# A four-part graph network kernel: gathers of two layers start with the landed table, biases move from one-row products to additions, a split is shared with ScalarE

## The chip, the cores and the metric

One Trainium2 chip, of which the kernel uses one core: TensorE (PE, with its weight loads PEld), VectorE (DVE), ScalarE (ACT), GpSimd (POOL) and SyncE (SP, which issues most transfers), with SBUF and PSUM. The metric is the device time of one execution in microseconds.

## The reference

Four graph layers, each added to a residual x (6250 nodes of 128 features) behind a layer norm and a ReLU, over 106,250 edges (src, dst) sorted by dst:

```
x = x + L0(h)   # hypergraph attention, two conv layers l = 0, 1: xt = x@W; softmax over hyperedges;
                #   eout = segment_sum(m1, col); nout = segment_sum(m2, row); out = LN(nout + bias)*gamma + beta
                #   x = tanh(out + x)
x = x + L1(h)   # messages relu([x[row], x[col]] @ mW1 + mb1) @ mW2 + mb2, segment_sum to col,
                #   relu(relu([x, agg] @ uW1 + ub1) @ uW2 + ub2)
x = x + L2(h)   # gated edge messages with an inner layer norm, segment_sum, upd @ W_out + b_out
x = x + L3(h)   # two graph attentions, edges forwards and backwards
```

Here h = relu(layer_norm(x)) before each part.

## The kernel before

Nodes lie in 49 blocks (NB) of 128, handled in 13 GROUPS of up to four blocks. X, H and ACC hold 49 blocks of 128 features in SBUF: the residual, the layer's input and the sums. Edges lie in 928 tiles of 128; four tiles make one of 232 groups (NG).

The program is a row of stages, and the edge sweeps among them are ORDER = "abafcdee": a, b, a, f are the two conv layers of L0 (l = 0: a to the hyperedges, b back to the nodes; l = 1: a again, then f, which also reads kept one-hots and bits from memory), c is L1, d is L2, e twice is L3. This text calls the two a sweeps a0 and a2. Ahead of each sweep a short stage makes a table of transformed rows in memory:

- l0_sp, l0_pe, l0_ac, l0_ve (lines 1871 to 1953): the table tab[TW] of conv layer l. SP loads five weights and biases into WT (lines 1872 to 1877; both layers use the same place, so layer 1's loads wait for the stage to begin) and stores 13 groups (L1886). PE's first product (L1892) waits for all five.
- l0_mid (1961 to 1987): between a and b (or a and f); makes the hyperedges' means, stored to memory by L1981 in one transfer; DVE clears ACC (L1977).
- l0_end (1989 to 2040): DVE multiplies each of four parts of blocks (PARTS) by gamma (L2008), adds beta (L2009), adds H (L2010), ACT takes the tanh; three norm statistics and ACT's normalisation (L585) go in turns with it.
- l1_sp, l1_pe, l1_ac, l1_ve (2059 to 2112): L1's table tab[256] (13 stores, L2068) and, in SBUF, the rows for the destination side, which DVE splits into three bfloat16 parts per group (mb1 added by L2109, then the four instructions of split_ve, L658 to L661). SP loads w1, w2, u1, u2 and three biases at its beginning (L2060 to L2065); PE's first product and DVE wait for all seven.
- u_pe, u_ve, u_ac (2140 to 2214): L1's update network; l2_* (2218 to 2271): L2's tables and a spill of X to memory (L2220, 1792 KB); v_pe, v_ve (2279 to 2324): L2's output product. In u and v the product with u2 or Wo is followed by a product of one row that adds the bias (times1, 2121 to 2126).

In a sweep, rows_po (L618 to L623) has POOL issue four indirect gathers per group (one tile each: 128 table rows) into a ring of groups: 10 deep in a, 8 in b, f and c. POOL waits only for the semaphore that says a ring place has been read (S.r; in a it is ACT's L899 that reads it). DVE makes one-hot matrices, PE sums by them, DVE adds the sums to ACC.

Between stages all five engines meet: each drains, counts up s_met and waits until all five have done so (pass_by counts up without waiting, and own makes an engine wait for its own last instruction):

```python
def meet(eng):
    met[eng.engine] = met.get(eng.engine, 0) + 1
    eng.drain().then_inc(s_met, 1)          # L152
    eng.wait_ge(s_met, 5 * met[eng.engine])
def pass_by(eng):
    met[eng.engine] = met.get(eng.engine, 0) + 1
    eng.drain().then_inc(s_met, 1)
```

An idle stretch that the profile ends with L152 so ended with another engine's arrival at such a meeting. There is a meeting between l0 and a, two between a and b or f, and one between l1 and c. At the first a, credit_po (L467), a set of GpSimd stores of its own, comes between l0 and the sweep.

Of the kernel before, what the change touches and what calls it, by code (L numbers as in the profile page):

```python
# [10 lines left out]
ALU = mybir.AluOpType  # L11
# [91 lines left out]
def build(nc, a, out):  # L103
# [5 lines left out]
    with ctx:  # L109
# [915 lines left out]
        def b_po(po, p):  # L1025
            at, ring = raised_before(p)
# [82 lines left out]
        def f_po(po, p):  # L1109
            at, ring = raised_before(p)  # L1110
# [116 lines left out]
        def c_po(po, p):  # L1227
            meet(po)
# [623 lines left out]
        Wc0, att = WT[:, 0:130], WT[:, 130:132]  # L1852
        bia, gam, bet = (WT[:, 140 + 128 * i:268 + 128 * i] for i in range(3))
# [16 lines left out]

        def l0_sp(sp, l):
            sp.dma_start(Wc0[:, 0:128], a["L0_gnn_W"][l]).then_inc(s_w0, 16)
            sp.dma_start(att, a["L0_gnn_att"][l].rearrange("(c p) -> p c", p=128),
                         allow_slow_non_contiguous=True).then_inc(s_w0, 16)
            sp.dma_start(bia, bcast(a["L0_gnn_bias"][l], 128)).then_inc(s_w0, 16)
            sp.dma_start(gam, bcast(a["L0_gnn_gamma"][l], 128)).then_inc(s_w0, 16)
            sp.dma_start(bet, bcast(a["L0_gnn_beta"][l], 128)).then_inc(s_w0, 16)
# [9 lines left out]
            for i in range(NGR - 4, NGR):  # L1887
                stored(sp, l, i)

        def l0_pe(pe, l):  # L1890
            pe.wait_ge(s_w0, 80 * (l + 1))
            pe.transpose(PS[:, 7, 0:128], Wc0[:, 0:128], ident[:, :]).then_inc(s_wt, 1)  # L1892
            pe.wait_ge(s_wtc, l + 1)
            pe.matmul(PS[:, 7, 0:2], W0t, att, start=True, stop=True).then_inc(s_wp, 1)
            z = N0 * l
            for t in range(N0 + 1):
# [7 lines left out]
                if t >= 1:  # L1904
# [5 lines left out]
                    if i >= 2:  # L1910
                        pe.wait_ge(s_ts, z + i - 1)
                    times(pe, wide(2 + 2 * (i % 2), n, w), n,
                          [(wk512(i % 2), Wc0[:, 0:129] if w == 129 else Wc0[:, 129:130])]).then_inc(s_pr, 1)

        def l0_ac(ac, l):
# [3 lines left out]
            for t in range(N0):  # L1919
# [4 lines left out]
                ac.activation(wk512(t % 2)[:, 0:128 * n], PS[:, t % 2, 0:128 * n], ACT.Copy).then_inc(s_ht, 1)  # L1924

        def l0_ve(ve, l):
# [6 lines left out]
            ve.tensor_copy(Wc0[:, 128:130], PS[:, 7, 0:2]).then_inc(s_wc, 1)  # L1933
# [55 lines left out]
        def l0_end_ve(ve, l):  # L1989
# [5 lines left out]
            def summed(i):  # L1995

                lo, hi = PARTS[i]
                for b in range(lo, hi):
                    last = ve.scalar_tensor_tensor(A[:, b, :], A[:, b, :], S2[:, b:b + 1], bia, ALU.mult, ALU.add)
# [3 lines left out]
            def added(i):  # L2003
# [4 lines left out]
                own(ve, "ve", ve.tensor_tensor(P, P, rep(gam, hi - lo), ALU.mult))  # L2008
                own(ve, "ve", ve.tensor_tensor(P, P, rep(bet, hi - lo), ALU.add))  # L2009
# [44 lines left out]
        SQT, SQU = (B2[:, 9420 + 512 * i:9932 + 512 * i].rearrange("p (b c) -> p b c", c=128) for i in range(2))  # L2054
# [4 lines left out]
        def l1_sp(sp):  # L2059
            sp.dma_start(c2(w1), two(a["L1_gnn_mW1"])).then_inc(s_w1, 16)  # L2060
            sp.dma_start(w2, a["L1_gnn_mW2"]).then_inc(s_w1, 16)
            sp.dma_start(c2(u1), two(a["L1_gnn_uW1"])).then_inc(s_w1, 16)
# [9 lines left out]
        def l1_pe(pe):  # L2072
            for t in range(NGR + 1):
# [29 lines left out]

        def l1_ve(ve):
# [11 lines left out]
        s_np = sem("normed_part")  # L2116
# [3 lines left out]

        def times1(pe, outs, n, HT, w, bias):

            for k in range(n):
                pe.matmul(outs[:, k, :], HT[:, 128 * k:128 * k + 128], w, start=True, stop=False)
                mm = pe.matmul(outs[:, k, :], one_row, bias[0:1, :], start=False, stop=True)
            return mm
# [13 lines left out]
        def u_pe(pe):  # L2140

            for t in range(NGR + 3):
# [17 lines left out]
                if f := staged(t, 3):  # L2160
# [4 lines left out]
                    times1(pe, slim(6 + i % 2, n), n, uDH[i % 2], u2, ub2).then_inc(s_ur, 1)  # L2165
# [19 lines left out]
        def u_ve(ve):  # L2185

            for t in range(NGR + 3):
# [73 lines left out]
        def l2_ve(ve):  # L2261

            for i, (b0, n) in enumerate(GROUPS):
# [5 lines left out]
                ve.tensor_tensor(SB[:, b0:b0 + n, :], wide(4, n, 256), rep(bsr[1], n), ALU.add).then_inc(s_tb2, 1)  # L2269

# [8 lines left out]
        def v_pe(pe):  # L2279
            for t in range(NGR + 1):  # L2280
# [5 lines left out]
                if f := staged(t, 1):  # L2286
# [4 lines left out]
                    times1(pe, slim(2 + i % 2, n), n, vH[i % 2], Wo, bob).then_inc(s_up, 1)  # L2291
# [403 lines left out]
```

## Time and profile before

| | us |
|---|---|
| median of the runs (3; 11420.74 to 11429.36) | 11423.58 |
| the profiled execution | 11428.81 |
| its span, first to last instruction | 11427.0 |
| POOL busy in it | 7501.8 (66%) |
| PE busy / PE weight loads | 8042.8 (70%) / 5923.8 (52%) |
| DVE busy | 7905.9 (69%) |
| ACT busy | 5676.6 (50%) |
| granted TensorE clock, mean | 0.688 |

A share over the whole span says little here, since the stages have different limits. The sweeps are a 1024 to 2192 us, b 2237 to 3405, a2 3517 to 4677, f 4720 to 5882, c 6040 to 7205, d 7335 to 8712, and the two e behind 8853; between them lie the short stages named above. A clock of 1.00 is TensorE at 2.4 GHz and 0.50 at 1.2 GHz; a value between them is a mean over a stretch that has both.

### The profile page before, as it was taken

The numbers are of one execution on the slowest core, as the hardware profiler recorded it, in microseconds if no ns is written. First come the engines' busy times: TensorE is split into PE (matmuls) and PEld (weight loads), VectorE is DVE, ScalarE is ACT, GpSimd is POOL, SyncE is SP. The second block draws the span as 40 slices with busy tenths as digits, with TensorE's granted clock in tenths as the row PEclk, the third lists the DMA queues.
The fourth block names the chain that finished last, engine by engine and source line by source line (L and its number), as shares of the span: only waits on it lengthen the run. The fifth ranks groups of instructions, "written<-read, shape, count | busy, mean of one in ns | idle before, by whom it ended". The sixth has DMA issues, their size and how long they took to land. (4 is left out here: it accounts for less than half of the span.)

```text
span 11427.0 us, 187407 instructions
## 1 busy us (share of the span) xinstructions
PE 8042.8 (70%) x47078; PEld 5923.8 (52%) x47078; DVE 7905.9 (69%) x33260; ACT 5676.6 (50%) x17089; POOL 7501.8 (66%) x7674
## 2 busy tenths in 40 slices
PE   7895777666665777666645555888888777767776
PEld 5674444444444444444434555666666444444444
DVE  8766888744447888644453222588886799979998
ACT  4553555454444555455551111366665566646665
POOL 2444777677775777677756777466663677747775
PEclk8776666655556666555557777899998666666666
DMA  1112222255652222488954444355553544444443
GB/s 17 9 20 50 55 55 55 65 136 135 136 127 56 56 55 55 126 215 212 211 140 130 131 131 131 109 155 154 154 153 100 136 139 138 138 116 139 139 137 114
DMA packets 713309, 1294.48 MB, mean 113 GB/s; under 512 B 197090, under 2 KB 369216, under 8 KB 711872
## 3 DMA queue, kind: packets, MB, share of 16 engines
q0 software_dynamic: 282368, 575.57, 24.7%
q1 hardware_dynamic: 389520, 612.10, 16.8%
q10 hardware_dynamic: 40368, 94.82, 2.1%
q8 instruction: 411, 6.73, 0.2%
q14 instruction: 642, 5.26, 0.2%
HBM read 1048.44 MB, written 233.37 MB: 112 GB/s over the span
## 5 line engine op out<-in xcount | busy, mean ns | idle before, releaser
L623 POOL DMA_INDIRECT WK<-tab,IDX x4640 | 4411.9, 951 | 1702.9 <-issue 1372.3
L1637 POOL DMA_INDIRECT B<-tab,IDX x1856 | 1780.2, 959 | 710.8 <-issue 529.2
L623 POOL DMA_INDIRECT H<-tab,IDX x928 | 880.2, 949 | 539.2 <-DVE H L1441 261.6
L1767 ACT ACTIVATE B<-B 128x33 f32<-128x33 f32 x5568 | 1210.7, 308 | 7.9
L1656 DVE TENSOR_REDUCE WK<-PS 128x4 f32<-128x1024 f32 x928 | 1130.3, 1219 | 91.7 <-PE PS L1782 85.2
L926 PE MATMUL PS<-B 128*128 128x130 f32 (+1 forms) x3712 | 777.7, 374 | 393.2 <-ACT B L899 393.1
L1815 PEld LDWEIGHTS PS<-B,H 128*128 128x128 f32 x3712 | 829.2, 333 | 377.5 <-issue 372.2
L1815 PE MATMUL PS<-B,H 128*128 128x132 f32 x3712 | 893.6, 435 | 177.3 <-DVE ACC L1669 177.3
L1782 PE MATMUL PS<-WK,B 27*128 27x512 bf16 x1856 | 690.0, 481 | 396.0 <-DVE WK L1656 386.7
L926 PEld LDWEIGHTS PS<-B 128*128 128x128 f32 x3712 | 661.8, 268 | 581.6 <-ACT B L899 581.6
L887 ACT ACTIVATE B<-PS,PICK 18x512 bf16<-18x512 f32 x464 | 357.3, 770 | 1138.2 <-PE PS L944 1116.3
L1243 DVE TENSOR_TENSOR WK<-PS,WK 128x512 f32<-128x512 f32 x232 | 160.4, 692 | 840.0 <-DMA WK<-tab,IDX 826.1
L985 PE MATMUL PS<-WK,B 128*128 128x129 f32 x1856 | 381.0, 370 | 509.2 <-ACT WK L1287 366.5
L463 POOL DMA_INDIRECT pieces<-WK,B x208 | 353.4, 1699 | 574.4 <-ACT WK L451 294.6
L1022 ACT ACTIVATE B<-WK 128x128 f32<-128x128 f32 x1856 | 588.7, 388 | 237.9 <-ACT B L698 93.6
L1287 ACT ACTIVATE WK<-WK 128x512 f32<-128x512 f32 x232 | 146.5, 631 | 968.6 <-DVE WK L1243 968.6
L985 PE MATMUL PS<-B 128*128 128x129 f32 x1856 | 467.8, 430 | 222.6 <-ACT B L1022 222.2
L985 PEld LDWEIGHTS PS<-WK,B 128*128 128x128 f32 x1856 | 329.7, 267 | 555.7 <-issue 555.1
L899 ACT ACTIVATE B<-WK 128x128 f32<-128x128 f32 x1856 | 584.6, 385 | 0.0
L985 PE MATMUL PS<-B,WK 128*128 128x129 f32 x1856 | 474.1, 435 | 138.0 <-ACT B L1022 135.4
L397 PEld LDWEIGHTS PS<-B,WK 128*128 128x128 f32 x3328 | 487.7, 234 | 115.1 <-issue 100.9
L985 PEld LDWEIGHTS PS<-B 128*128 128x128 f32 x1856 | 403.6, 320 | 274.0 <-ACT B L1022 273.4
(476 smaller groups left out, 19980.9 us busy)
## 6 DMA issues: line engine op xcount, KB each, us to landing
H<-onehots SPq DMA_DIRECT2D x232, 768.0 KB
B<-onehots SPq DMA_DIRECT2D x232, 384.0 KB
onehots<-B ACTq DMA_DIRECT2D x232, 384.0 KB
WK<-tab,IDX POOLq DMA_INDIRECT x4640
onehots<-WK SPq DMA_DIRECT2D x232, 256.0 KB
B<-onehots SPq DMA_DIRECT2D x232, 256.0 KB
WK<-onehots SPq DMA_DIRECT2D x232, 256.0 KB
onehots<-B SPq DMA_DIRECT2D x232, 128.0 KB
```

Source lines behind the costliest of these rows:

```text
L397: mm = pe.matmul(PS[:, 4 + x % 2, 64 * (t // TC):64 * (t // TC) + 64], OHL[x % 2][:, t, :], PROD[x % 2][:, t, :, :].rearrange("p i w -> p ...
L623: po.indirect_dma_start(out=G[:, g % n, k, :], out_offset=None, in_=table, in_offset=bass.IndirectOffsetOnAxis(ap=IDX[:, idx, t:t + 1], ax ...
L887: ac.activation(aETb[:, r % 2, :], PS[0:18, 2 + r % 2, :], ACT.Identity, bias=abi[0:18, :], scale=asc[0:18, :]).then_inc(S.n1, 1)
L899: i = ac.activation(aR[:, r % 2, k, 0:128], aG[:, g % 10, k, 0:128], ACT.Copy, scale=aEW[:, r % 2, k:k + 1])
L926: mm = pe.matmul(aAG(r, k // 2)[:, 0:n], aOH[:, g % 10, k, :], aR[:, r % 2, k, 0:n], start=k % 2 == 0, stop=k % 2 == 1)
L985: mm = pe.matmul(AG(r, k // 2), OH[:, r, k, :], R[:, r % n, k, 0:129], start=k % 2 == 0, stop=k % 2 == 1)
L1022: i = ac.activation(bR[:, r % 2, k, 0:128], bG[:, r, k, 0:128], ACT.Copy, scale=bEW[:, r % 2, k:k + 1])
L1637: po.indirect_dma_start(out=eG[:, g % 5, k, :], out_offset=None, in_=tab[TW3], in_offset=bass.IndirectOffsetOnAxis(ap=IDX[:, o, t:t + 1], ...
L1656: ve.tensor_reduce(eM2[:, g, b:b + 2, 2 * i:2 * i + 2, 1] if isinstance(g, int) else eM2[:, bass.ds(g, 1), b:b + 2, 2 * i:2 * i + 2, 1].re ...
L1767: i = ac.activation(eR[:, q, k, 33 * h:33 * h + 33], eG[:, g % 5, k, 33 * h:33 * h + 33], ACT.Copy, scale=eEX[:, r, 4 * k + h:4 * k + h + 1])
L1782: mm = pe.matmul(PS[:, b + h, :], eSEL[:, b + h, :], eET[:, r, 512 * i:512 * i + 512], start=True, stop=True)
L1815: mm = pe.matmul(eAG(k // 2), eSTo[:, r, k // 4, 128 * (k % 4):128 * (k % 4) + 128], eR[:, r % 2, k, 0:132], start=k % 2 == 0, stop=k % 2 ...
```

## The change

- In a, b, f and c, POOL passes the meeting by and waits for the stores of the table (the last four of the 13, or the one of the means). One meeting of all engines per l0, and the one behind l1, go. credit_po moves into l0. The tiles HT0 of l0 move out of the memory that the gathers fill.
- L0's weights have a place for each layer; layer 1's are loaded at the end of layer 0's l0_sp. L1's w1, w2 and u1 are loaded in f's SP program at its ninth group; PE waits for these three alone.
- beta is added to H in four parts during b and f (shifted_ve), no longer to ACC in l0_end.
- In l1, DVE only adds mb1 per group, into ACC. Afterwards ACT makes eight copies and DVE eight subtractions over quarters of the blocks, in turns, and DVE clears ACC at the end; before, the clearing stood at the start.
- times1 becomes times. In u DVE adds ub2 in PSUM ahead of the ReLU; in v's place DVE adds bob to X in four parts during l2, and X's spill goes behind the eleventh store of l2.

The diff, cut to its core:

```diff
@@ f_sp
+                if g == 8:
+                    sp.dma_start(c2(w1), two(a["L1_gnn_mW1"])).then_inc(s_w1, 16)
+                    sp.dma_start(w2, a["L1_gnn_mW2"]).then_inc(s_w1, 16)
+                    sp.dma_start(c2(u1), two(a["L1_gnn_uW1"])).then_inc(s_w1, 16)
         def a_po(po, p):
-            meet(po)
+            pass_by(po)
+            for i in range(NGR - 4, NGR):
+                stored(po, p // 2, i)
             at, ring = raised_before(p)
...
         def b_po(po, p):
+            pass_by(po)
+            po.wait_ge(s_eod, 16)
             at, ring = raised_before(p)
...
+        def shifted_ve(ve, j, l):
+
+            if j in (24, 32, 40, 48):
+                lo, hi = PARTS[j // 8 - 3]
+                ve.wait_ge(s_w0, 80 * (l + 1))
+                ve.tensor_tensor(H[:, lo:hi, :], H[:, lo:hi, :], rep(bet[l], hi - lo), ALU.add)
...
             def body(j, u):
+                shifted_ve(ve, j, 0)
...
         def f_po(po, p):
+            pass_by(po)
+            po.wait_ge(s_eod, 32)
...
             def body(j, u):
+                shifted_ve(ve, j, 1)
...
         def c_po(po, p):
-            meet(po)
+            pass_by(po)
+            for i in range(NGR - 4, NGR):
+                stored(po, 2, i)
...
+        w0 = [WT[:, 756 * l:756 * l + 524] for l in range(2)]
+        HT0 = [B2[:, 8000 + 512 * i:8512 + 512 * i] for i in range(2)]
...
         def l0_sp(sp, l):
-            sp.dma_start(Wc0[:, 0:128], a["L0_gnn_W"][l]).then_inc(s_w0, 16)
...
-            sp.dma_start(bet, bcast(a["L0_gnn_beta"][l], 128)).then_inc(s_w0, 16)
+            if l == 0:
+                l0_weights_sp(sp, 0)
...
             for i in range(NGR - 4, NGR):
                 stored(sp, l, i)
+            if l == 0:
+                l0_weights_sp(sp, 1)
@@ l0_end_ve
-                own(ve, "ve", ve.tensor_tensor(P, P, rep(gam, hi - lo), ALU.mult))
-                own(ve, "ve", ve.tensor_tensor(P, P, rep(bet, hi - lo), ALU.add))
+                own(ve, "ve", ve.tensor_tensor(P, P, rep(gam[l], hi - lo), ALU.mult))
@@ l1_pe
-                    pe.wait_ge(s_w1, 112)
+                    pe.wait_ge(s_w1, 48)
...
+        def split_ac(ac):
+
+            ac.wait_ge(s_sq1, NGR)
+            for q, i in ((0, 0), (1, 0), (0, 1), (2, 0), (1, 1), (3, 0), (2, 1), (3, 1)):
+                whole, p, rest = sq_part(q)
+                if i:
+                    ac.wait_ge(s_sb, (1, 2, 4, 6)[q])
+                ac.activation(p[i], rest if i else whole, ACT.Copy).then_inc(s_sa, 1)
+
         def l1_ve(ve):
-            ve.memset(flat(ACC[:, :, :]), 0.0)
             ve.wait_ge(s_w1, 112)
             for i, (b0, n) in enumerate(GROUPS):
                 ve.wait_ge(s_ta1, i + 1)
-                ve.tensor_tensor(SQT[:, 0:n, :], wide(2 + 2 * (i % 2), n, 256)[:, :, 128:256], rep(mb1, n),
+                ve.tensor_tensor(ACC[:, b0:b0 + n, 0:128], wide(2 + 2 * (i % 2), n, 256)[:, :, 128:256], rep(mb1, n),
                                  ALU.add).then_inc(s_sq1, 1)
-                ve.wait_ge(s_sq1, i + 1)
-                split_ve(ve, lambda k: SQ3[:, b0:b0 + n, k, :], SQT[:, 0:n, :], SQU[:, 0:n, :])
+            for q, last_ in ((0, 0), (1, 0), (0, 1), (2, 0), (1, 1), (3, 0), (2, 1), (3, 1)):
+                whole, (p0, p1, p2), rest = sq_part(q)
+                if last_:
+                    ve.wait_ge(s_sa, (3, 5, 7, 8)[q])
+                    ve.tensor_tensor(p2, rest, p1, ALU.subtract).then_inc(s_sb, 1)
+                else:
+                    ve.wait_ge(s_sa, (1, 2, 4, 6)[q])
+                    if q >= 2:
+                        ve.wait_ge(s_sb, (3, 5)[q - 2])
+                    ve.tensor_tensor(rest, whole, p0, ALU.subtract).then_inc(s_sb, 1)
+            own(ve, "ve", ve.memset(flat(ACC[:, :, :]), 0.0))
@@ u_pe, v_pe
-                    times1(pe, slim(6 + i % 2, n), n, uDH[i % 2], u2, ub2).then_inc(s_ur, 1)
+                    times(pe, slim(6 + i % 2, n), n, [(uDH[i % 2], u2)]).then_inc(s_ur, 1)
...
-                    times1(pe, slim(2 + i % 2, n), n, vH[i % 2], Wo, bob).then_inc(s_up, 1)
+                    times(pe, slim(2 + i % 2, n), n, [(vH[i % 2], Wo)]).then_inc(s_up, 1)
@@ u_ve
-                    ve.scalar_tensor_tensor(X[:, b0:b0 + n, :], slim(6 + i % 2, n), 0.0, X[:, b0:b0 + n, :], ALU.max,
+                    F = slim(6 + i % 2, n)
+                    own(ve, "ve", ve.tensor_tensor(F, F, rep(ub2, n), ALU.add))
+                    ve.scalar_tensor_tensor(X[:, b0:b0 + n, :], F, 0.0, X[:, b0:b0 + n, :], ALU.max,
@@ l2_sp, l2_ve
-            sp.wait_ge(s_ux, NGR)
-            sp.dma_start(xs[:, 128 * XK:], xf[:, 128 * XK:]).then_inc(s_xs, 16)
...
+                if i == 10:
+                    sp.wait_ge(s_bob, 4)
+                    sp.dma_start(xs[:, 128 * XK:], xf[:, 128 * XK:]).then_inc(s_xs, 16)
...
+                if i in (3, 5, 7, 9):
+                    lo, hi = PARTS[(i - 3) // 2]
+                    ve.wait_ge(s_np, (i - 3) // 2 + 1)
+                    ve.tensor_tensor(X[:, lo:hi, :], X[:, lo:hi, :], rep(bob, hi - lo), ALU.add).then_inc(s_bob, 1)
@@ @block.gpsimd (one meet less per l0 layer on each other engine too, and one behind l1)
-                meet(po)
                 if l == 0:
+                    po.wait_ge(s_ts, 1)
                     credit_po(po)
                 a_po(po, 2 * l)
-                meet(po)
                 meet(po)
```

## Rows read from the trace of the kernel before

**Rows 1.** Windows a0, b, c, u, d, v: PE, PEld, DVE, ACT, POOL; clock; DMA.

```profile
1024.00:2192.00 1168.00, 840.52 (x5026) 559.95 (x5026) 979.64 (x6400) 595.44 (x1818) 885.18 (x928) 0.65 0.25 55
2237.00:3405.00 1168.00, 767.80 (x3920) 542.00 (x3920) 529.09 (x3233) 581.11 (x1612) 885.17 (x927) 0.52 0.59 135
6040.00:7205.00 1165.00, 652.62 (x4784) 592.81 (x4785) 285.96 (x715) 153.51 (x247) 882.14 (x928) 0.73 0.47 132
7214.70:7287.60 72.90, 71.62 (x420) 57.47 (x420) 44.49 (x182) 29.57 (x64) 9.43 (x5) 0.93 0.06 26
7390.00:8748.90 1358.90, 1134.43 (x6745) 932.38 (x6744) 1214.00 (x4798) 885.38 (x2031) 838.43 (x885) 1.00 0.51 151
8766.00:8851.30 85.30, 85.16 (x265) 62.25 (x265) 35.95 (x169) 22.34 (x51) 7.84 (x4) 0.50 0.13 50
```

**Rows 2.** Timeline of POOL, first gathers: start, us, instruction [idle before <-releaser].

```profile
1024.23 1.16 POOL L623 DMA_INDIRECT WK<-tab,IDX  x1 [79.40 <-SPq L152]
...
2237.24 1.00 POOL L623 DMA_INDIRECT WK<-tab,IDX  x1 [44.35 <-DVEq L152]
...
3517.36 1.06 POOL L623 DMA_INDIRECT WK<-tab,IDX  x1 [63.70 <-SPq L152]
...
6040.23 1.02 POOL L623 DMA_INDIRECT WK<-tab,IDX  x1 [58.61 <-DVEq L152]
```

**Rows 3.** Timeline of SP's queue: the stores ahead of a0, b, a2, c.

```profile
984.70 13.14 SPq L1886 DMA_DIRECT2D tab<-WK  x10
...
2221.75 0.36 SPq L1981 DMA_DIRECT2D tab<-ACC  x1
...
3481.25 18.17 SPq L1886 DMA_DIRECT2D tab<-WK  x13
...
6000.55 33.26 SPq L2068 DMA_DIRECT2D tab<-WK  x13
```

**Rows 4.** DMA issues: xcount, KB each, median us to landing.

```profile
tab<-WK SPq DMA_DIRECT2D x24, 264.0 KB, 3.0
...
tab<-ACC SPq DMA_DIRECT2D x2, 1650.0 KB, 8.3
...
tab<-WK SPq DMA_DIRECT2D x12, 256.0 KB, 2.3
```

**Rows 5.** Waits of PE in a0, DVE in b, f, c: total us, times, longest.

```profile
PE PS L944 <- DMA WK<-tab,IDX: 33.7, 61, 2.4
...
DVE WK L1052 <- DMA WK<-tab,IDX: 562.7, 227, 5.5
...
DVE B L704 <- DMA bits<-B: 385.7, 210, 6.9
...
DVE WK L1243 <- DMA WK<-tab,IDX: 826.1, 228, 7.5
```

**Rows 6.** Timeline of DVE at a0's start, of PE at the second l0's.

```profile
1023.38 3.45 DVE L854 TENSOR_SCALAR B<-iof,LOW 128x128 f32<-128x128 f32 x16 [3.93 <-SPq L152]
...
3474.47 0.45 PE L1892 MATMUL PS<-ident,WT 128*128 128x128 f32 x1 [60.31 <-DMA WT<-in_L_gnn_beta]
```

**Rows 7.** Groups of DVE instructions in the first l0_end: busy us, mean ns.

```profile
L2009 DVE TENSOR_TENSOR ACC<-ACC,WT 128x1536 f32<-128x1536 f32 (+1 forms) x4 | 7.2, 1791 | 0.1
```

**Rows 8.** Groups of instructions in l1, its products on PE.

```profile
L1845 PE MATMUL PS<-WT,WK 128*128 128x256 f32 x98 | 26.1, 412 | 11.4 <-DMA WT<-in_L_gnn_ub 4.9 <-ACT WK L2095 4.2 <-DVE B L2109 2.3
```

**Rows 9.** Timeline of PE in u: a block with its bias, products without.

```profile
7241.06 0.48 PE L2125 MATMUL PS<-WT,IDX 1*128 1x128 f32 x2
...
7241.89 0.48 PE L2125 MATMUL PS<-WT,IDX 1*128 1x128 f32 x2
...
7244.46 1.06 PE L1845 MATMUL PS<-WT,WK 128*128 128x128 f32 x8
```

**Rows 10.** Timeline of DVE in v: two groups.

```profile
8800.01 0.69 DVE L2319 TENSOR_TENSOR X<-X,PS 128x512 f32<-128x512 f32 x1 [0.94 <-PE PS L2125]
...
8806.54 0.69 DVE L2319 TENSOR_TENSOR X<-X,PS 128x512 f32<-128x512 f32 x1 [4.65 <-PE PS L2125]
```

More of the change, by code:

```diff
@@ L1849, in wk512 @@
             return WK[:, 512 * i:512 * i + 512]
-        Wc0, att = WT[:, 0:130], WT[:, 130:132]
-        bia, gam, bet = (WT[:, 140 + 128 * i:268 + 128 * i] for i in range(3))
+        w0 = [WT[:, 756 * l:756 * l + 524] for l in range(2)]
+        Wc0, att = [w[:, 0:130] for w in w0], [w[:, 130:132] for w in w0]
+        bia, gam, bet = ([w[:, 140 + 128 * i:268 + 128 * i] for w in w0] for i in range(3))
+        HT0 = [B2[:, 8000 + 512 * i:8512 + 512 * i] for i in range(2)]
         W0t = wk512(2)[:, 0:128]
@@ L1869, in stored, with l0_weights_sp @@
             eng.wait_ge(s_st[m % 4], 16 * (m // 4 + 1))
-        def l0_sp(sp, l):
-            sp.dma_start(Wc0[:, 0:128], a["L0_gnn_W"][l]).then_inc(s_w0, 16)
[L1873 to L1876, printed above, removed]
-            sp.dma_start(bet, bcast(a["L0_gnn_beta"][l], 128)).then_inc(s_w0, 16)
+        def l0_weights_sp(sp, l):
+            sp.dma_start(Wc0[l][:, 0:128], a["L0_gnn_W"][l]).then_inc(s_w0, 16)
+            sp.dma_start(att[l], a["L0_gnn_att"][l].rearrange("(c p) -> p c", p=128),
+                         allow_slow_non_contiguous=True).then_inc(s_w0, 16)
+            sp.dma_start(bia[l], bcast(a["L0_gnn_bias"][l], 128)).then_inc(s_w0, 16)
+            sp.dma_start(gam[l], bcast(a["L0_gnn_gamma"][l], 128)).then_inc(s_w0, 16)
+            sp.dma_start(bet[l], bcast(a["L0_gnn_beta"][l], 128)).then_inc(s_w0, 16)
+        def l0_sp(sp, l):
+            if l == 0:
+                l0_weights_sp(sp, 0)
             sp.wait_ge(s_rfc, l + 1)
@@ L1888, in l0_sp @@
                 stored(sp, l, i)
+            if l == 0:
+                l0_weights_sp(sp, 1)
         def l0_pe(pe, l):
             pe.wait_ge(s_w0, 80 * (l + 1))
-            pe.transpose(PS[:, 7, 0:128], Wc0[:, 0:128], ident[:, :]).then_inc(s_wt, 1)
+            pe.transpose(PS[:, 7, 0:128], Wc0[l][:, 0:128], ident[:, :]).then_inc(s_wt, 1)
             pe.wait_ge(s_wtc, l + 1)
-            pe.matmul(PS[:, 7, 0:2], W0t, att, start=True, stop=True).then_inc(s_wp, 1)
+            pe.matmul(PS[:, 7, 0:2], W0t, att[l], start=True, stop=True).then_inc(s_wp, 1)
             z = N0 * l
@@ L1912, in l0_pe @@
                     times(pe, wide(2 + 2 * (i % 2), n, w), n,
-                          [(wk512(i % 2), Wc0[:, 0:129] if w == 129 else Wc0[:, 129:130])]).then_inc(s_pr, 1)
+                          [(HT0[i % 2], Wc0[l][:, 0:129] if w == 129 else Wc0[l][:, 129:130])]).then_inc(s_pr, 1)
         def l0_ac(ac, l):
@@ L1923, in l0_ac @@
                     ac.wait_ge(s_pr, z + t - 1)
-                ac.activation(wk512(t % 2)[:, 0:128 * n], PS[:, t % 2, 0:128 * n], ACT.Copy).then_inc(s_ht, 1)
+                ac.activation(HT0[t % 2][:, 0:128 * n], PS[:, t % 2, 0:128 * n], ACT.Copy).then_inc(s_ht, 1)
         def l0_ve(ve, l):
@@ L1932, in l0_ve @@
             ve.wait_ge(s_wp, l + 1)
-            ve.tensor_copy(Wc0[:, 128:130], PS[:, 7, 0:2]).then_inc(s_wc, 1)
+            ve.tensor_copy(Wc0[l][:, 128:130], PS[:, 7, 0:2]).then_inc(s_wc, 1)
             z = N0 * l
@@ L1998, in summed @@
                 for b in range(lo, hi):
-                    last = ve.scalar_tensor_tensor(A[:, b, :], A[:, b, :], S2[:, b:b + 1], bia, ALU.mult, ALU.add)
+                    last = ve.scalar_tensor_tensor(A[:, b, :], A[:, b, :], S2[:, b:b + 1], bia[l], ALU.mult, ALU.add)
                 own(ve, "ve", last)
@@ L2053, in build @@
         SQ3 = SQP.rearrange("p (b i c) -> p b i c", i=3, c=128)
-        SQT, SQU = (B2[:, 9420 + 512 * i:9932 + 512 * i].rearrange("p (b c) -> p b c", c=128) for i in range(2))
+        SQU = B2[:, 9420:9420 + 25 * 128].rearrange("p (b c) -> p b c", c=128)
         TS1 = [wk512(4 + i).rearrange("p (b c) -> p b c", c=128) for i in range(4)]
@@ L2059, in l1_sp @@
         def l1_sp(sp):
-            sp.dma_start(c2(w1), two(a["L1_gnn_mW1"])).then_inc(s_w1, 16)
-            sp.dma_start(w2, a["L1_gnn_mW2"]).then_inc(s_w1, 16)
-            sp.dma_start(c2(u1), two(a["L1_gnn_uW1"])).then_inc(s_w1, 16)
             sp.dma_start(u2, a["L1_gnn_uW2"]).then_inc(s_w1, 16)
@@ L2102, in l1_ac, with sq_part @@
                                   ACT.Copy).then_inc(s_ta1, 1)
+        s_sa, s_sb = sem("split_copied"), sem("split_rest")
+        def sq_part(q):
+            lo, hi = PARTS[q]
+            return ACC[:, lo:hi, 0:128], [SQ3[:, lo:hi, i, :] for i in range(3)], SQU[:, 12 * (1 - q % 2):12 * (1 - q % 2) + hi - lo, :]
+        def split_ac(ac):
[5 more added lines that the diff above has]
+                ac.activation(p[i], rest if i else whole, ACT.Copy).then_inc(s_sa, 1)
         def l1_ve(ve):
-            ve.memset(flat(ACC[:, :, :]), 0.0)
             ve.wait_ge(s_w1, 112)
@@ L2119, in build @@
                  14: (2, 0, 4), 15: (2, 4, 8), 16: (2, 8, 12)}
[L2121 to L2126, printed above, removed]
         def normed_ac(ac, n, q, lo, hi):
@@ L2509, in _ @@
                 meet(po)
-            meet(po)
             c_po(po, 4)
@@ L2543, in _ @@
                     bits_ve(ve)
-                meet(ve)
                 a_ve(ve, 2 * l, l)
@@ L2553, in _ @@
             l1_ve(ve)
-            meet(ve)
             c_ve(ve, 4)
@@ L2575, in _ @@
                 l0_ac(ac, l)
-                meet(ac)
                 a_ac(ac, 2 * l)
@@ L2584, in _ @@
             l1_ac(ac)
-            meet(ac)
+            split_ac(ac)
             c_ac(ac, 4)
@@ L2616, in _ @@
                     pick_pe(pe)
-                meet(pe)
                 a_pe(pe, 2 * l, l)
@@ L2624, in _ @@
             l1_pe(pe)
-            meet(pe)
             c_pe(pe, 4)
@@ L2649, in _ @@
                 meet(sp)
-                meet(sp)
                 l0_mid_sp(sp, l)
@@ L2659, in _ @@
             l1_sp(sp)
-            meet(sp)
             meet(sp)
```

2 lines of the change are left out of this document (1 added, 1 removed).

## The prediction

> **What bounds the kernel now.** I read the table of stages first [rows 1]. In the five sweeps that the change touches, GpSimd issues 928 gathers, and the stage takes about 928 times one gather's pitch: 1168 us over 928 is 1.26 us. No other engine is full there: DVE, the next in a0, is busy 980 of 1168 us, TensorE 841. The list of who waits then agrees [rows 5]: in c DVE waits 826 us for gathers, in b 563. So the end of such a sweep is the first gather plus about 1168 us, and what counts is when that first gather starts. Next come the GpSimd rows at each start [rows 2]: it stands idle for 44 to 79 us until a drain of the meeting (L152) of SyncE or VectorE, not until data. Between sweeps, short stages are bound by other things: u and v by TensorE [rows 1], layer 1's table by DVE's split and by its weights.
>
> **Gathers begin with the landed table.** Each stage: last store's issue, its landing, and the distance to the first gather.
> - a0: the last store of the table is issued by 984.70 + 13.14 = 997.8 [rows 3] and lands 3.0 us later [rows 4]: 1000.9. The first gather is at 1024.23 [rows 2]. Gain **23.3**. The consumers get less: DVE's first one-hots start at 1023.38 after 3.93 us for that meeting [rows 6], most of it GpSimd's credit stage, now done earlier: about 3.9 sooner. The gathers so run 19.4 us (four groups of 5.03, 1168 over 232) further ahead into a ring of ten. In the steady state TensorE waits only 33.7 us in 61 waits for gathers [rows 5], so the consumers keep pace with little to spare; their own slack, 980 of 1168 us on DVE, is some 0.4 us per group at most, enough to win 19 us back over 50 to 100 of the 232 groups. I take the full 23.3, with 3.9 as the lower bound (the ring full from the start and never caught up).
> - b: one store of the means is issued at 2221.75 + 0.36 and lands after 8.3 [rows 3, 4]: 2230.4, against the first gather at 2237.24: **6.5**, after a little for the wait. The meeting here waits for DVE's clearing of the accumulators; the consumers have half their time idle [rows 1, 5] and follow.
> - a2: stores end 3481.25 + 18.17 + 3.0 = 3502.4 against 3517.36: **14.5**, bounds 4 and 15 as in a0.
> - f: built as b and worth 6.5 at its start, but DVE waits 386 us in 210 waits for the kept bits from memory [rows 5], so gathers aren't alone in setting its end. I take **3** of -2 to 6.5.
> - c (layer 1): three things in one start. Before, the first gather is 6040.23 and the 13 stores run from 6000.55 for 33.26 us [rows 2, 3]: 12 steps of 2.77 us, paced by the DVE split that frees PSUM. With the split behind the stage TensorE paces it: 26.1 us of its products by 13 groups is 2.0 us [rows 8], some of it at the lower clock, 2.16 with the transposes: 12 x 0.61 = 7.3. The weights, loaded in f, no longer hold TensorE for 4.9 [rows 8]. The last landing (6033.8 + 2.3 [rows 4]) is 4.1 ahead of the first gather, 0.5 of which stays: 3.6. Sum **15.8**, bounds 11 and 17. What it adds lies in c's beginning: eight ACT copies and eight DVE subtractions of about 1.8 us each (as L2009's tiles, [rows 7]), alternating, and a clearing of 6517 elements, 7 us at L2009's pace (an estimate), that stood in the weights' shadow. c's consumers start 7 us later than now, so 23 us further behind the gathers, under the 40 us that the ring of eight holds; with 826 us of waiting in c they catch up within ten groups. If that cover were gone, it would cost those 7.
>
> **Weights of layer 1 of the hypergraph, loaded early.** TensorE's first product stands until 3474.47 for the last of five loads [rows 6]; the meeting is over at about 3467.7. About 1.1 of it remains: **5.7** (3 to 6.8). SyncE issues the same five loads behind a0's stores, where its queue has nothing due.
>
> **Norm's shift in the passes.** L2009 is four additions of 1.79 us [rows 7] in each of two ends, a chain of DVE and ACT in turns. Half of 7.2 lies on the path: **3.6 each, 7.2 in all** (3.6 to 14). The additions now stand in b and f, where DVE waits 563 and 386 us [rows 5]; without that cover they'd cost 7.2 each.
>
> **One-row products.** In u TensorE is busy 71.6 of 72.9 us [rows 1]. The products with a bias take 0.83 us per block (two passes and two one-row passes), while eight products without a bias take 1.06 [rows 9]: per group 3.3 becomes about 1.0. DVE becomes the bound: 44.5 us busy [rows 1] and 13 more additions of 0.69 (a pass over such a tile, [rows 10]) are 53.5, with fill and tail 59: gain 14. Layer 2's table then gets four additions of 1.8 us in DVE's gaps (cover: its stage is bound by TensorE), and the spill of X (1792 KB; a store of 1650 KB lands in 8.3 us [rows 4]) moves ahead of the last two stores: -1 to -3. I take **11** (0 to 15). In v the clock was 0.50 throughout and a group takes 6.53 us [rows 1, 10]; with 4 transposes and 8 products it is about 2.8 (an estimate: 1.06 doubled and 0.7), DVE with its statistics 3.1: 13 groups make 40, with fill and the last statistics 47 instead of 86: 39. The table stage behind may then see more of the low clock, 0 to 19: I take **36** (20 to 41).
>
> **The sum.** 23.3 + 6.5 + 14.5 + 3 + 15.8 + 5.7 + 7.2 + 11 + 36 = **123 us**. The profiled execution took 11428.8 us (span 11427.0 and 1.8 around it), 5 us over the median of 11423.6. 11428.8 - 123 is 11306, the median's own 11301; I say **11304**. The terms at their low ends give about 3.9 + 6 + 4 - 2 + 11 + 3 + 3.6 + 0 + 20 = 50, at their high ends about 145.
>
> **The rivals.**
> 1. **The head start is given back in a0 and a2.** For it: TensorE's waits for gathers there are short, and the granted clock of 0.65 isn't fixed; a ring that fills puts the end on the consumers, and only their 3.9 and 4 count. Against: gathers run at their pitch through all of a0, with no wait for a free buffer. Loses 30: gain 93, **11333**.
> 2. **The clock falls in u, or v's slow clock goes on behind it.** u has 0.93 now [rows 1]; with fewer products it may lie at 0.50, as v, and then its transposes and remaining products take twice as long and u keeps 5 us a group. Gain 123 - 11 - 16 = 96, **11330**. The Trainium skill, page "TensorE: Matmul & The Clock Gate", section "What's actually happening", says that the throttled state is the default and that activity releases it. By that rule thinner work in u and v makes this rival likelier; v speaks against it as a whole, since TensorE was busy 85.2 of 85.3 us there at 0.50 [rows 1].
> 3. **Slower: d loses its full clock.** d runs at 1.00 from 7390 to 8749, with TensorE busy 1134 of 1359 us [rows 1]. If u and the table behind it leave d in the mixed clock of a (0.65), its matmuls take about 1.2 to 1.35 times as long, TensorE's 1134 become 1360 to 1530, and d grows by up to 170 us. It decides from the point where d's granted clock is under about 0.8. Then 11428.8 - 123 + 170 = **11476**. Against: layer 2's table, dense and unchanged, lies between u and d.
> 4. **Gathers suffer from DVE's work beside them.** They now start while DVE clears an accumulator (7 us by the estimate above), splits or makes one-hots, and each could stand that long. The Trainium skill, page "DMA: Bandwidth & Descriptors", section "SWDGE vs HWDGE vs iDMA", says that DVE in its two-port modes locks GpSimd out of the memory in which it writes descriptors. By that a gather would wait out a clearing or a 1.8 us pass. The rows speak against much of it: with DVE busy 84% of a0 a gather keeps 1.26 us. Four stages with a clearing beside the gathers lose 4 x 7 = 28 at most: gain 95, **11334**.
> 5. **The meeting wasn't what held GpSimd.** Then a drain or a late wait keeps it, gathers gain nothing, and only u, v, the weights and the shift remain: 55 to 60 us, **11370**.
>
> **How the numbers follow.** Forecast (11285 to 11325) 0.60; rival 1 0.14; rival 2 0.12; rival 3 0.05; rival 4 0.04; rival 5 0.05. Rivals 1, 2 and 4 overlap the edge of the forecast and can add up, to about 11360. The range is 11280 to 11365: it leaves out rival 3, most of 5 and a tail of the sum. A difference of 0.2%, 23 us, is about what a measurement of this kernel can tell from no change. All but rival 3 are over it; with half of rival 3's size ending near zero, and something unforeseen in the rest: faster 0.92, within 0.2% 0.04, slower 0.04.
>
> **What would show it.** First gathers at about 1001, and then 6.5, 14, 6 and 35 us after the marks named above; stages a, b and c still 1165 to 1170 us from their first to their last gather (longer by the lost head start under rival 1, with GpSimd waiting for the consumers' ACT copies L899); TensorE's products in u and v about one third, with DVE waiting no more for them; d at clock 1.00 and as long as now; c's DVE waiting less for gathers in its first ten groups and not after. A gather over 1.3 us beside clearings would speak for rival 4. The forecast is wrong as a whole if a sweep's end doesn't follow its first gather.

## The result and the profile after

The changed kernel takes 11291.08 us, median of 4 runs (11284.41 to 11301.47), against 11423.1 of the kernel before (four runs by now): 0.9888, 95% interval 0.9876 to 0.9900, a gain of 132 us. The forecast was 11304, with a sum of 123. Its profiled execution took 11297.06 us (span 11295.3).

Where the gain lies is read from marks that both timelines have: the end of the last DVE addition to ACC in each sweep. From one such end to the next a stage takes its start, its 928 gathers and its tail. The table is worked out from these marks, with a second execution of each kernel (the last part of the experiments), which shows what varies by itself.

| stage, to the end of sweep | before | before, second | changed | changed, second | forecast gain | gain, second pair |
|---|---|---|---|---|---|---|
| a0 (from the program's start) | 2214.7 | 2214.4 | 2196.3 | 2192.5 | 23.3 | 21.9 |
| b | 1200.3 | 1200.2 | 1197.3 | 1196.6 | 6.5 | 3.6 |
| a2 (with l0_end and l0's weights) | 1282.7 | 1284.6 | 1259.5 | 1258.6 | 23.8 | 26.0 |
| f | 1207.2 | 1193.7 | 1192.2 | 1191.9 | 3 | 1.8 |
| c (with l0_end and l1) | 1309.6 | 1310.0 | 1292.1 | 1292.9 | 19.4 | 17.1 |
| d (with u and l2) | 1551.4 | 1557.1 | 1545.3 | 1541.5 | 11 | 15.6 |
| first e (with v) | 1344.5 | 1343.6 | 1299.5 | 1296.7 | 36 | 46.9 |
| second e and the end | 1316.5 | 1313.1 | 1313.1 | 1313.2 | 0 | -0.1 |
| sum | 11427.0 | 11416.6 | 11295.3 | 11283.9 | 123 | 132.7 |

The answers to [rows 2], the timeline of GpSimd of the changed kernel at the starts of a0, b, a2 and c (start, us, instruction, idle before and who ended it), with the last gather of b and of c:

```profile
1005.25 1.07 POOL L623 DMA_INDIRECT WK<-tab,IDX  x1 [60.16 <-DVE NV L1969]
...
2211.66 0.95 POOL L623 DMA_INDIRECT WK<-tab,IDX  x1 [37.55 <-SPq L152]
...
3383.62 0.95 POOL L623 DMA_INDIRECT WK<-tab,IDX  x1 [0.30 <-issue]
...
3470.69 1.02 POOL L623 DMA_INDIRECT WK<-tab,IDX  x1 [40.35 <-SPq L152]
...
5959.01 1.96 POOL L623 DMA_INDIRECT WK<-tab,IDX  x1 [40.63 <-SPq L152]
...
7127.57 0.95 POOL L623 DMA_INDIRECT WK<-tab,IDX  x1 [0.30 <-issue]
```

Ahead of b, a2 and c the profile names L152 as the end of the wait, though GpSimd now waits there only for its own earlier meetings and for the stores; the idle stretch begins behind the sweep before, so part of it is still a meeting. What counts is the start. And a0 has to be read from its own beginning, for the setup ahead of it took 3.8 us longer in this execution. The first DVE instruction of l0, before and after:

```profile
972.52 0.17 DVE L1927 MEMSET ACC<- 128x128 f32 x1
```

```profile
976.36 0.17 DVE L1956 MEMSET ACC<- 128x128 f32 x1
```

From there the first gather follows after 51.7 us before [rows 2] and 28.9 after: 22.8 of gain. In the second executions it is 48.7 and 28.9, 19.8 of gain, so this term is known only to about 3 us.

The answers to [rows 1], windows of b, c, u, d and v of the changed kernel (us, then PE, PEld, DVE, ACT, POOL busy with counts, granted clock, DMA share, GB/s):

```profile
2212.00:3384.00 1172.00, 766.16 (x3920) 541.85 (x3920) 542.39 (x3238) 584.48 (x1614) 889.37 (x928) 0.52 0.57 135
5959.00:7129.00 1170.00, 652.98 (x4786) 593.66 (x4786) 304.68 (x727) 163.00 (x254) 886.98 (x928) 0.72 0.46 132
7137.40:7197.60 60.20, 43.36 (x312) 40.85 (x313) 52.52 (x197) 30.46 (x67) 10.68 (x5) 0.89 0.00 1
7300.00:8659.00 1359.00, 1136.37 (x6740) 934.09 (x6741) 1212.30 (x4785) 886.12 (x2023) 841.75 (x889) 1.00 0.51 152
...
8682.80:8728.00 45.20, 29.35 (x169) 26.78 (x170) 35.33 (x170) 23.76 (x57) 9.32 (x4) 0.73 0.25 96
```

Three things are to be seen. In u TensorE is no longer full, and DVE is the busiest engine (52.5 of 60.2 us). d is as it was, at 1.00. And v runs at 0.73 instead of 0.50, which no forecast had. In b, POOL is busy 889.4 us for 928 gathers instead of 885.2 for one gather less: gathers have become longer there.

In the timeline of the changed kernel they are found. DVE and GpSimd at the second of the four additions in b:

```profile
2362.19 1.75 DVE L1044 TENSOR_TENSOR H<-H,WT 128x1536 f32<-128x1536 f32 x1
```

```profile
2360.80 0.95 POOL L623 DMA_INDIRECT WK<-tab,IDX  x1 [0.30 <-issue]
2362.05 2.72 POOL L623 DMA_INDIRECT WK<-tab,IDX  x1 [0.30 <-issue]
2365.07 0.95 POOL L623 DMA_INDIRECT WK<-tab,IDX  x1 [0.30 <-issue]
```

The addition ends at 2363.94; the gather beside it ends 0.83 later, at 2364.77, and has taken 2.72 us instead of 0.95. The other three of b end 0.82 behind their additions, after 1.63, 1.96 and 2.08 us. No other gather of b takes over 1.5.

### The profile page after: what moved, and what is told of

Its sections match the earlier page's. It is cut to its first block and busy times, and to the rows that moved or that the text cites. A ratio compares the mean times of both kernels' runs of the same rounds, so it can differ in the third digit from the quotient of the medians.

```text
span 11295.3 us, 186975 instructions
## 1 busy us (share of the span) xinstructions
PE 7922.8 (70%) x46882; PEld 5846.9 (52%) x46882; DVE 7895.6 (70%) x33233; ACT 5713.9 (51%) x17097; POOL 7515.0 (67%) x7674
```

## Experiments

My theory was that the parts add up, each at its own place: a sweep ends about 1168 us behind its first gather, so a gather that starts earlier is worth its head start, less what DVE's new passes cost the gathers beside them; and the one-row products carry u and v. The rivals were that head starts are given back by a full ring, that the gain of f and the clock in v belong to one execution, and that long gathers have another cause.

### The parts

**Gathers alone.** The changed kernel with only its first part; weights, shift, split and one-row products as before:

```diff
-    pe.wait_ge(s_w1, 48)          # and w1, w2, u1 loaded in l1_sp, layer 1's five in its own l0_sp
+    pe.wait_ge(s_w1, 112)
-    shifted_ve(ve, j, l)          # beta added in l0_end
-    split_ac(ac)                  # DVE splits within each group
-    times(pe, ...)                # times1 in u and v
```

> The changed kernel with only its first part kept: gathers begin with the landed table; weights, norm shift, layer 1's split and the one-row products stand as in the kernel before. Theory (each sweep's end follows its first gather): a0 gains 22 to 23 us, b 6 to 7, a2 14 to 15, c about 4 (the split still paces its table), and f 6.5 at its start; b's gathers from first to last take 1168 us as before, since no additions stand beside them. Together 52 to 56 us, 11367 to 11371; if f's consumers also end 9 us closer to its last gather, as in the changed kernel, 11358 to 11362. Rival (the ring fills in a0 and a2 and the head start is given back): their gathers take 10 to 20 us longer from first to last, total gain 20 to 35, 11388 to 11403.

Measured: 0.9953 of the kernel before (0.9937 to 0.9970), 11372.84 against 11433.75 on that chip. Its profiled execution ended at 11365.4, and its stages against the second execution of before are a0 -15.7 (here l0 began 3.3 us later than there), b -6.9, a2 -13.7, f -6.0, c -4.8. From first to last gather: a0 1167.7, b 1168.1, a2 1159.9, f 1160.2, c 1164.7, all as before. The head start is kept in full; the ring isn't the limit. Rival 1 of the prediction falls.

**All but the gathers.** The changed kernel with the meetings ahead of a, b, f and c back on all engines:

```diff
-            pass_by(po)
-            for i in range(NGR - 4, NGR):
-                stored(po, p // 2, i)
+            meet(po)
```

> The changed kernel without its first part: GpSimd waits for the meeting of all engines again ahead of a, b, f and c. Theory (the parts add up): it loses what the kernel with the first part alone gains in a0, b, a2 and f, 45 to 55 us, and in c more than 4, since the split, now behind the table's stores, stands before the meeting: the first gather of c waits for about 22 us of split and clearing. Together 65 to 80, 11356 to 11371. Rival (the other parts carry the gain and the gathers' head start is worth little): loses under 30, below 11320.

Measured: 0.9949 (0.9933 to 0.9966), so this kernel has lost some 64 to 68 of about 132 us; by stages against the second execution of the changed kernel a0 +19.4, b +10.6, a2 +13.2, f +5.3, c +15.3, together 63.8. That is just under the 65 to 80 expected. By the medians the two halves gain 60.9 and 64.3, together 125 of about 132, so the parts add up within the intervals. b took 1174.8 us from first to last gather here, with its four additions: the long gathers don't depend on the head start.

**One-row products back.**

```diff
-    times(pe, slim(2 + i % 2, n), n, [(vH[i % 2], Wo)])
+    times1(pe, slim(2 + i % 2, n), n, vH[i % 2], Wo, bob)     # u likewise; no additions of ub2 and bob
```

> The changed kernel with the one-row products back in u and v (and the spill of X at its old place). Theory A (in v the one-row products themselves go with the low clock): u is 73 us again, v 87 at a granted clock of 0.50, loss 12 and 38, 11340. Theory B (the low clock in v of the kernel before was that run's, and comes or goes by itself): v at 1.00 takes 13 groups of 5.05 and its tail, 70 us; loss 12 and 20, 11322.

Measured: 0.9942 (0.9925 to 0.9958). From d's last addition to the end of the first e 1341.9 us, as before (1344.5, 1343.6), and 42 to 45 more than the changed kernel; d with u 1550.9, 6 to 9 more. v's window, in the columns of the windows above:

```profile
8691.00:8774.00 83.00, 83.00 (x259) 60.49 (x258) 34.86 (x159) 22.33 (x51) 7.05 (x3) 0.50 0.13 52
```

TensorE full for 83 us and the clock at 0.50 throughout, as in [rows 1]; the kernel with the gathers alone, which has these products too, shows 0.51 over 88 us. Theory A, then: with one-row products the low clock is there in all three kernels that have them and whose v was read. Whether it is their thinness or only more work that does it is the next one's question.

**Each product twice.**

```diff
-                    times(pe, slim(2 + i % 2, n), n, [(vH[i % 2], Wo)])
+                    times_twice(pe, slim(2 + i % 2, n), n, vH[i % 2], Wo)   # two products, both start=True; u likewise
```

> The changed kernel with each product in u and v made twice in full (the second overwrites the first): as many matmuls as with one-row products, but none of one row. Theory A (the one-row products go with the low clock in v, whatever their number): v comes to a clock of 1.00 within some 20 us as in the changed kernel; 16 products and 4 transposes take about 2.6 us a group, under DVE's 3.1, so u and v are as long as in the changed kernel, 11291 within 5 us. Theory B (busier TensorE behind d stays at the low clock, whatever it multiplies): v at 0.50 throughout, 16 products 4.2 us and transposes 1.1, 5.3 a group, v 20 to 25 us longer, 11311 to 11316.

Measured: 0.9894 (0.9877 to 0.9910), and v, with as many matmuls as before the change:

```profile
8693.00:8740.00 47.00, 35.06 (x265) 33.10 (x265) 35.83 (x171) 22.68 (x54) 9.32 (x4) 0.86 0.24 92
```

and the groups of TensorE in that window (busy, mean ns, idle before and its releaser), beside those of the kernel with one-row products:

```profile
L2173 PE MATMUL PS<-WGT,WK 128*128 128x128 f32 x98 | 20.5, 293 | 7.1 <-DVE X L2375 5.3 <-ACT WK L2356 1.7
L2174 PE MATMUL PS<-WGT,WK 128*128 128x128 f32 x98 | 19.7, 284 | 0.0
```

```profile
L2174 PE MATMUL PS<-WGT,IDX 1*128 1x128 f32 x98 | 38.8, 497 | 0.0
L2173 PE MATMUL PS<-WGT,WK 128*128 128x128 f32 x98 | 37.2, 483 | 0.0
```

Theory A again, for v: 98 more full products cost v about 2 us (47.0 in the window against 45.2), since the clock came back to 1.00 early in v and DVE set the pace. In every kernel here the clock falls 14 to 17 us before d's last sum. With one-row products it then stays low for 99 to 102 us, until v is through; without them it first comes back to 1.00 3 to 6 us behind d's last sum, some 20 us after it fell. It is one-row products, not more products, that go with the long low clock here. They don't bring the clock down, though: in u of the kernel before the same pairs ran at 0.93 [rows 1], from a start at 1.00. And the second product here also overwrites instead of adding, which was not separated.

The Trainium skill, page "TensorE: Matmul & The Clock Gate", section "What's actually happening", says that a throttled clock is the default and activity releases it. In v of the kernel before TensorE was full for 85 us [rows 1] and the clock stayed low, so that sentence alone doesn't tell what v does; no run here measured what the chip counts as activity.

The median, 11308.89, lies above theory A's 11291 within 5 and close to theory B's 11311. But the kernel before took 11 us more on this chip, too, and the five sweeps of the profiled execution, which u and v don't touch, took 13.7 us more from first to last gather than those of the changed kernel. So v's clock and window decide, not the median.

**The shift back in the layers' ends.**

```diff
+                own(ve, "ve", ve.tensor_tensor(P, P, rep(bet[l], hi - lo), ALU.add))   # l0_end; no shifted_ve
```

> The changed kernel with beta added in the ends of the two hypergraph layers again, no additions in b and f. Theory (a DVE addition with both inputs in SBUF holds up the gather that is being issued beside it): b's 928 gathers take 1168 us again instead of 1172 to 1175, f's 1160 instead of 1163 to 1166, with no gather over 1.5 us; each end is 3.6 longer. Together -7 to -10 and +7: as long as the changed kernel within 3 us. Rival (b and f vary by so much by themselves): b and f as in the changed kernel, 7 us longer as a whole.

Measured: 11288.43, 0.9885 (0.9869 to 0.9902), no different from the changed kernel. b 1166.7 and f 1160.9 from first to last gather, no gather over 1.5 us in either; the starts of a2 and c are 4.5 and 4.1 us longer than in the first profile of the changed kernel. This part of the change won about 4 in each end and lost 4 to 5 in b and 3 in f.

**The split within each group again.**

```diff
+                split_ve(ve, lambda k: SQ3[:, b0:b0 + n, k, :], SQT[:, 0:n, :], SQU[:, 0:n, :])   # no split_ac
```

> The changed kernel with layer 1's split made by DVE within each group again. Theory: the table's stores are paced by DVE (2.77 us a group instead of 2.16), so c's first gather comes 7 to 10 us later; in return c's first eight gathers have no subtractions beside them and c's gathers take 1164 to 1165 us instead of 1168.6. Net 3 to 6 us longer than the changed kernel. Rival (the eight long gathers come from something else at c's start, such as the destination loads): c's gathers stay at 1168 and the loss is 7 to 10.

Measured: 11294.96, 0.9893 (0.9876 to 0.9909). c's first gather comes 122.7 us behind f's end instead of 113.7, 9.0 later; from first to last gather it takes 1165.8 instead of 1168.6. The 13 stores of the table leave every 2.79 us instead of 1.99, 9.5 over twelve steps. So the split shared with ScalarE is worth 9.0 at the table and gives 2.8 back to the gathers.

### What holds a gather

**Small additions.** 49 additions of one block in place of four:

```diff
-            if j in (24, 32, 40, 48):
+            if 24 <= j < 24 + NB:
```

> The changed kernel with the shift in 49 additions of one block (128 elements, about 0.2 us) instead of four of 12 or 13 blocks. Theory (a gather stands until the addition beside it ends): a gather can stand at most 0.2 us, no gather over 1.5 us, b's gathers take 1168 to 1170 instead of 1172 to 1175, f's 1160 to 1162; 5 to 8 us shorter than the changed kernel. Rival (it is the amount of DVE traffic that slows gathers): b and f as in the changed kernel.

Measured: 11280.66, 0.9883 (0.9867 to 0.9900); b 1169.2, f 1160.2 from first to last gather. An addition takes 0.28 us, the longest gather 1.26. DVE adds as many elements as before and takes even longer for them in all (49 times 0.28 us, 13.7, against about 7.1), so it isn't the amount; but five gathers of b took 0.30 us longer, where 0.2 at most was expected.

**The split in small pieces, too.**

```diff
-            lo, hi = PARTS[q]
+            b0, n = GROUPS[q]      # 13 pieces, 26 subtractions; four buffers for the rest
```

> As the kernel with 49 small additions, and layer 1's split, too, by 13 groups instead of quarters: 26 subtractions of 0.7 us in place of eight of 1.8. Theory: a gather stands until the subtraction beside it ends; a stream of short ones holds each of some eleven gathers 0.35 us on average, 3.9 together, so c is about as now (1168), the rest as with small additions alone. Rival (short operations let gathers through between them): c's gathers 1165 to 1166, 2 to 3 us shorter still.

Measured: 11270.80, 0.9870 (0.9854 to 0.9887); c 1164.9 from first to last gather. The rival was right: short subtractions cost almost nothing, though they stand back to back. The timelines of GpSimd at c's start, first of the changed kernel (second execution), then of this one (second execution):

```profile
5953.68 1.96 POOL L623 DMA_INDIRECT WK<-tab,IDX  x1 [41.13 <-SPq L152]
5955.95 1.29 POOL L623 DMA_INDIRECT WK<-tab,IDX  x1 [0.31 <-issue]
5957.54 1.58 POOL L623 DMA_INDIRECT WK<-tab,IDX  x1 [0.30 <-issue]
5959.42 1.56 POOL L623 DMA_INDIRECT WK<-tab,IDX  x1 [0.30 <-issue]
```

```profile
5942.43 1.03 POOL L623 DMA_INDIRECT WK<-tab,IDX  x1 [40.52 <-SPq L152]
5943.76 1.42 POOL L623 DMA_INDIRECT WK<-tab,IDX  x1 [0.30 <-issue]
5945.49 0.95 POOL L623 DMA_INDIRECT WK<-tab,IDX  x1 [0.30 <-issue]
5946.75 0.95 POOL L623 DMA_INDIRECT WK<-tab,IDX  x1 [0.30 <-issue]
```

and DVE beside the third gather of the latter:

```profile
5945.49 0.72 DVE L2163 TENSOR_TENSOR B<-ACC,B 128x512 f32<-128x512 f32 x1
5946.14 0.68 DVE L2159 TENSOR_TENSOR B<-B 128x512 bf16<-128x512 f32 x1
```

With eight subtractions of 1.8 us the first eight gathers take 1.29 to 1.96; with 26 of 0.7 only the second takes more than 1.2. From the third on a gather begins together with a subtraction, two subtractions to a gather, and takes 0.95 though subtractions run beside it all the while.

**Other operations.** In b eight additions, so that beta comes in doubled; in f, in place of the shift, which is left out there, four passes with one input:

```diff
+            if l == 1 and j in (24, 32, 40, 48):
+                ve.tensor_scalar(H[:, lo:hi, :], H[:, lo:hi, :], 0.0, None, ALU.add)
```

> The changed kernel with the shift in b added twice (eight additions instead of four, so beta comes in doubled), and in f, in its place, four operations on the same tiles with one SBUF input and a constant (beta of the second layer is left out). Theory (an operation with two SBUF inputs holds the gather beside it until it ends): b has eight gathers over 1.5 us and takes 1176 to 1182; f has none and takes 1160 to 1161. Rival 1 (any DVE pass of that length holds gathers): f has four long gathers, 1163 to 1166. Rival 2 (it isn't the additions): b as with four, 1172 to 1175.

Measured in one execution (11279.35): b has its eight long gathers (1.49 to 2.61 us) and takes 1175.5 from first to last, so a long addition costs 0.9 to 1.0 us. But f has four longer gathers as well, 1.25 to 1.57, and takes 1161.9, between none and the four additions. One of them, DVE and then GpSimd:

```profile
4853.20 0.95 DVE L1048 TENSOR_SCALAR H<-H 128x1536 f32<-128x1536 f32 x1
```

```profile
4853.49 1.47 POOL L623 DMA_INDIRECT WK<-tab,IDX  x1 [0.30 <-issue]
```

The pass ends at 4854.15 and the gather 0.81 later; the other three end 0.12 behind their passes. So one input doesn't free the gather: my theory was too narrow. The pass of one input costs less because it is over after 0.95 us instead of 1.75, and because most of its gathers end 0.12 behind it, while beside additions and subtractions the distance is 0.82 or 0.83 throughout (0.90 for c's first); the two were not separated. A clearing does free it. Of the changed kernel, DVE and GpSimd behind c's split:

```profile
5973.66 5.49 DVE L2161 MEMSET ACC<- 128x6517 f32 x1 [1.31 <-issue]
```

```profile
5974.74 0.95 POOL L623 DMA_INDIRECT WK<-tab,IDX  x1 [0.30 <-issue]
5976.00 0.95 POOL L623 DMA_INDIRECT WK<-tab,IDX  x1 [0.30 <-issue]
5977.26 0.95 POOL L623 DMA_INDIRECT WK<-tab,IDX  x1 [0.30 <-issue]
```

The Trainium skill, page "SBUF — State Buffer", section "SBUF: two separate sides", says that a DVE pass in a two-port mode, or one with two inputs in SBUF beside a GpSimd operation that reads SBUF, and the GpSimd operation hold a shared pair of ports in turns, each for a whole instruction. The long gathers beside additions and beside the one-input pass agree with it in part, since each ends at a fixed distance, 0.12 or 0.82 us, behind the pass. The gathers of 0.95 us that run beside two-input subtractions from start to end don't agree with "a whole instruction"; what a gather holds, and when, no run here measured.

### The same kernels once more

Before, changed and small pieces were run again on one chip, with no edits.

> The kernel before, once more. The last sum of f ended 22.7 us behind its last gather in the profile of the kernel before and 11 to 14 us in all kernels since, with and without the gathers' head start and the shift. Theory (9 us of f's gain were that one execution's): here, too, it ends 11 to 14 behind. Rival (something common to all changed kernels shortens f's end): 20 to 24 again. The first gather of a0 lies within 1010 to 1032, as far as the setup ahead of it varies.

Measured: 11418.45; f's last addition ends 12.0 us behind its last gather, not 22.7. So 10.7 of the 13.4 us by which f differs between the two executions of the kernel before are this tail, and the 15.0 that the table's first pair would give is really 1.8. The first gather of a0 was at 1024.1, while in the changed kernels it varies from 994 to 1010.

> The changed kernel once more, beside the kernel with small pieces on the same chip: b 1172 to 1175, f 1163 to 1166 and c 1168.6 from first to last gather. 0.9885 to 0.989 of the kernel before.

> The kernel with small pieces once more: b 1169 to 1170, f 1160 to 1161, c 1165: 10 to 12 us under the changed kernel by the stages, 0.9875 to 0.988 of the kernel before. If the small pieces only move the waiting elsewhere, no difference from the changed kernel beside it.

Measured: 11284.92 (11279.34 to 11286.88), 0.9882 (0.9865 to 0.9898), and 11273.75 (11264.52 to 11279.55), 0.9872 (0.9856 to 0.9889). From first to last gather b 1171.0 and 1168.8, f 1163.6 and 1159.8, c 1168.6 and 1164.9: 9.8 us together, of 11 between the medians. The intervals against the kernel before overlap, but the two sets of runs on this chip barely touch. The kernel with small pieces is the fastest of the study, 145 us under the kernel before beside it.

## Why the prediction was right, point by point

- **Gathers begin with the landed table.** Right in mechanism and size. a0 23.3 foreseen, 22.8 and 19.8 from l0's beginning; c's start 19.4 foreseen, 135.4 to 113.7, 21.7 measured. The head start was not given back anywhere: the consumers won it back as the prediction had it from [rows 5].
- **b: the mis-sized term.** At its start 6.8 was gained of 6.5 foreseen (45.3 from last to first gather before, 38.5 after). But the stage gained only 3.0 to 3.6. The step that failed is "The additions now stand in b and f, where DVE waits": I took DVE's idle time for a cover, and the cover that was missing was GpSimd's, whose gathers set the sweep and stand while a long DVE pass runs. The price is 3 to 4 us in b (up to 7 in one execution), about 3 in f and 4 in c, 10 to 11 in all, so rival 4 was true beside the forecast at less than half of its 28. But its clearings held no gather (they take 5.49 us, not the 7 estimated); additions and subtractions did.
- **Norm's shift.** 7.2 foreseen in the ends, 8.6 found there by the kernel without this part, and 7 to 8 of it lost in the passes. As a part it was worth nothing.
- **Weights.** l0's second start: with gathers alone it is 87.3 us, with weights as well 81.6 (the kernel without the shift): 5.7, as foreseen.
- **f.** 3 foreseen, 1.8 by the second pair, but not for the reason given: the kept bits were to take the rest of the 6.5, and the kernel with the gathers alone kept 6.0 of it. What took it were the long gathers, about 3 us. The near hit is luck, and the first pair's 15.0 is one execution's tail.
- **Layer 1's split.** 7.3 for the pace, 4.9 for the weights and 3.6 for the meeting were foreseen. Without the split's part the start is 9.0 longer, more than 7.3, mainly since the stores leave every 1.99 us and not every 2.16. c's consumers do start later and this costs nothing, as foreseen. (L1's table is tab[128] in the kernel, not tab[256].)
- **u.** DVE became the bound. u's last sum comes 52.9 us behind c's end instead of 67.0, 14 gained as foreseen; from there to d's first gather it takes 58 to 60 instead of 53.7, 4 to 6 lost of 1 to 3 foreseen. Together 8 to 10 of 11, and 6 to 9 by the stage of the kernel with the one-row products back. The table's 15.6 has 5.6 us in it by which d's stage differs between the two executions of the kernel before: in the second u had the low clock for 27 us instead of 10.
- **v: the other mis-sized term.** 36 foreseen, 45 to 47 found. v's last sum comes 36 to 37 us behind d's end instead of 80.9, 44 to 45 gained of 39 foreseen. I had taken 3.1 us a group for DVE, which sets the pace there now; the 35.95 us of DVE in [rows 1] are 2.8 for each of 13 groups, which makes about 4. The table behind v, for which I had taken 3 off, lost nothing. What the returned clock is worth was not measured apart: DVE waits only 2.0 us for TensorE in v. Rival 2 expected the clock to move against the change: in u it fell a little, from 0.93 to 0.89, and u gained its 14 all the same; in v it rose. Rival 3 didn't occur: d stayed at 1.00 and at 1376 to 1377 us from first to last gather in all kernels.

The two errors, some 10 us lost to long gathers and some 10 gained in v, nearly cancel, so the sum came out closer than its parts: that is luck.

## What to carry to other kernels

An engine that has idle time is not a cover if another engine, the one that sets the stage, can be held by what is put there: look for what the bounding engine shares with it, and cut long passes beside it into short ones. A wait for everybody can be replaced by a wait for the data where the profile shows an engine idle until a meeting and its transfers long landed. Before a term is read off one pair of profiles, a second execution of both kernels shows which stages move by themselves.

## What was not expected of the hardware

- A gather that is held by a DVE pass over SBUF ends 0.82 us (with one input mostly 0.12) behind the pass's end: it took 2.72 us instead of 0.95 beside an addition of 1.75, 1.25 to 1.57 beside a one-input pass of 0.95, 0.95 beside a clearing of 5.49, and mostly 0.95 among subtractions of 0.7 that stand back to back.
- With pairs of a full and a one-row product v stayed at a granted clock of 0.50 (the 1.2 GHz level) with TensorE full for 83 to 85 us, in three kernels; two full products in place of each pair had 0.86, as many matmuls in little over half the time. In u, where the clock stood at 1.00 when they began, the same pairs ran at 0.93.
